# Decoder tail on one Trainium2 core: row lists of the last batch from one-hot products, kept experts' first weights loaded in the mixer, four gather buffers cleared before the block, rows weighted directly behind silu

## The reference

```python
logits = x @ gate_weight.T                      # 128 experts, 80 of them masked out
probs = softmax(where(old_to_new == -1, -inf, logits))
top_v, top_i = top_k(probs, 8); top_v = top_v / top_v.sum(-1)
flat_e = old_to_new[top_i]                      # kept expert of each (token, choice)
pos = running count of its expert, in token order
valid = pos < 192                               # capacity of an expert
gate_up = rows_of_expert @ gate_up_proj[e].T    # 512 -> 384
out = (silu(g) * u) @ down_proj[e].T            # 192 -> 512
final[token] += out * top_v   where valid
x = layernorm(x + final)
```

## Time and profile before

| | us |
|---|---|
| median of 3 timed runs | 2152.34 |
| lowest, highest | 2149.24, 2153.65 |
| the profiled execution's own time | 2148.72 |
| its span | 2147.0 |
| PE busy | 1748.3 (81%) |
| DVE busy | 1482.3 (69%) |
| POOL busy | 1083.6 (50%) |
| ACT busy | 957.9 (45%) |
| granted TensorE clock, mean | 0.887 |

### The profile page before, as it was taken

How to read it: one execution, slowest core, us unless ns; L and a number is a source line. 1 busy time by engine, 2 the same in 40 slices (tenths; PEclk the granted TensorE clock), 3 DMA queues, 4 the chain that set the end, 5 groups by cost and what they waited for, 6 DMA issues and landing times. The chain is left out here.

```text
span 2147.0 us, 34548 instructions
## 1 busy us (share of the span) xinstructions
PE 1748.3 (81%) x9164; PEld 1395.6 (65%) x9165; DVE 1482.3 (69%) x2836; ACT 957.9 (45%) x1867; POOL 1083.6 (50%) x816
## 2 busy tenths in 40 slices
PE   4898989347999999999998898697851179999990
PEld 3566665236889888888887556464531178888880
DVE  4466867764777888887886323857679557777774
ACT  4354452312444444444443323535333157777773
POOL 1000715464667667667676000036357757777763
PEclk9898989666999999999999899887865589999995
DMA  8011011034888888888986623131010469999967
GB/s 325 27 40 59 20 59 40 1 102 141 209 212 212 206 220 225 219 219 216 232 228 134 224 39 59 44 74 59 1 59 1 170 179 256 258 248 258 256 150 255
DMA packets 138551, 318.72 MB, mean 148 GB/s; under 512 B 30840, under 2 KB 31320, under 8 KB 136824
## 3 DMA queue, kind: packets, MB, share of 16 engines
q1 hardware_dynamic: 71448, 201.68, 27.1%
q0 software_dynamic: 64752, 112.04, 26.9%
q10 hardware_dynamic: 2288, 4.29, 0.5%
HBM read 238.61 MB, written 97.62 MB: 157 GB/s over the span
## 5 line engine op out<-in xcount | busy, mean ns | idle before, releaser
L98 POOL DMA_INDIRECT tab_rows<-pair,slot x256 | 313.9, 1226 | 450.7 <-DVEq L752 299.3
L90 PE MATMUL gu<-wgu_h,xgT_h 128*128 x648 | 233.5, 360 | 7.2 <-DVE xgT_l L1428 3.6
L1253 POOL DMA_INDIRECT xg<-x_rows,ids x167 | 191.6, 1148 | 62.3 <-issue 48.5
L90 PE MATMUL gu<-wgu_l,xgT_h 128*128 x648 | 219.4, 339 | 0.0
L90 PE MATMUL gu<-wgu_h,xgT_l 128*128 x648 | 218.3, 337 | 0.0
L1308 ACT ACTIVATE ysb<-yp,wts 128x512 f32<-128x512 f32 x160 | 110.3, 689 | 144.6 <-PE yp L1535 144.6
L90 PE MATMUL guk<-xgT_hk,wgu_hk 128*128 128x192 f32 x576 | 161.2, 280 | 0.0
L90 PE MATMUL guk<-xgT_lk,wgu_hk 128*128 128x192 f32 x576 | 158.4, 275 | 0.0
L1298 ACT ACTIVATE sg<-gu 128x192 f32<-128x192 f32 x162 | 53.7, 331 | 234.4 <-PE gu L90 234.4
L90 PE MATMUL guk<-xgT_hk,wgu_lk 128*128 128x192 f32 x576 | 158.2, 275 | 0.0
L1428 DVE TENSOR_TENSOR xgT_l<-tpx,xgT_h 128x512 fp32r<-128x512 f32 x163 | 112.2, 688 | 54.4 <-ACT xgT_h L1294 52.2
(11 more groups left out here) (500 smaller groups left out, 5108.1 us busy)
## 6 DMA issues: line engine op xcount, KB each, us to landing
wgu_sb<-in_wgu SPq DMA_DIRECT2D x64, 768.0 KB
wgu_sbk<-in_wgu SPq DMA_DIRECT2D x48, 768.0 KB, 4.4
wd_sb<-in_wd SPq DMA_DIRECT2D x64, 256.0 KB
wd_sbk<-in_wd SPq DMA_DIRECT2D x48, 256.0 KB, 5.2
ct<-in_ctxT SPq DMA_DIRECT2D x8, 1024.0 KB, 4.9
wd_sb<-in_wd SPq DMA_DIRECT2D x64, 128.0 KB
wd_sbk<-in_wd SPq DMA_DIRECT2D x48, 128.0 KB, 5.8
odd_rows<-zero SPq DMA_DIRECT2D x1, 4352.0 KB, 15.5
```

The source lines that it names most:

```text
L90: i = nc.tensor.matmul(out, left(k), right(k), start=(start and k == 0 and m == 0), stop=(k == ops - 1 and m == 2))
L98: nc.gpsimd.indirect_dma_start(out=tab, out_offset=bass.IndirectOffsetOnAxis(ap=s["slot"][:, n:n + 1].bitcast(U32), axis=0), in_=s["pair"] ...
L1253: nc.gpsimd.indirect_dma_start(out=xg[:, t % G, :], out_offset=None, in_=x, in_offset=bass.IndirectOffsetOnAxis(ap=ids[:, t:t + 1].bitcast ...
```

## The change

Four edits. (1) In the last batch no slot numbers and no scatter: all four tiles are routed at once; `own` is the one-hot of each of the 32 choices, and for each choice n two products, `spots[:, n, :]` (a one-hot of the position, 192 wide) transposed times `parts[:, n, :, :]` (the one-hot of the expert times five values: 1, token number, and the weight in three bf16 pieces), sum up on PE to the list entries of the last batch. The table holds the first three batches; it is loaded by SP, transposed as before, and both are added into `ids` and `wts` inside `mixer_two`. (2) SP loads experts 0 to 2 of `kept_experts` inside `mixer_two`, as soon as the last attention output is out; the buffers live over both blocks. (3) Gather buffers 0 to 3 are a tensor that lives over both blocks and is cleared behind the spots; 4 to 7 are cleared at the head of `kept_experts`, and only the gathers into them wait for it. (4) In ACT's loop both `weighted` stand directly behind silu, ahead of `h_upper` and `rest_upper`.

```diff
+def kept_weights(sp, d, s, e, gate_up, down):
+    loaded = s["kept_loaded"][e % 2]
+    if e >= 2:
+        sp.wait_ge(loaded, e // 2 * 48)
+    sp.dma_start(gate_up, d["wgu1"][e * P:(e + 1) * P, :, :]).then_inc(loaded, 16)
+    sp.dma_start(down[:, 0, :], d["wd1"][e * INTER:e * INTER + P, :]).then_inc(loaded, 16)
+    sp.dma_start(down[0:IR, 1, :], d["wd1"][e * INTER + P:(e + 1) * INTER, :]).then_inc(loaded, 16)
@@ kept_experts, SP
-            for e in range(E1):
+            for e in range(NR, E1):
...
@@ kept_experts, POOL
-            scatter(nc, tab, s, E1 * REG1 - 1, s_lot, BT - 1)
             def gather(t):
                 if t >= GK:
                     pool.wait_ge(s_xT, t - GK + 1)
+                elif t >= G and t % 2 == 0:
+                    pool.wait_ge(s_clear, (t - G) // 2 + 1)
...
-            pool.wait_ge(s_tab, 3)
@@ kept_experts, ACT, step
                         silu(g + (n + 1) // NF, (n + 1) % NF)
+                    weighted(g, 2 * n, not first or n >= G // 2)
+                    weighted(g, 2 * n + 1, not first or n >= G // 2)
+                    if not (last and n + 1 >= NF):
                         h_upper(g + (n + 1) // NF, (n + 1) % NF)
-                    weighted(g, 2 * n, not first or n >= G // 2)
-                    if not (last and n + 1 >= NF):
                         rest_upper(g + (n + 1) // NF, (n + 1) % NF)
-                    weighted(g, 2 * n + 1, not first or n >= G // 2)
...
-            act.wait_ge(s_lot, SCAT)
-            nc.scalar.dma_start(lot[:, :, :].rearrange("t n o -> t (n o)"),
-                                tab.rearrange("(r n) o -> r (n o)", n=P)[0:T1, :]).then_inc(s_rows, 16)
@@ kept_experts, DVE
-            nc.vector.memset(xg[:, :, :], 0.0).then_inc(s_tab, 1)
+            for n in range((GK - G) // 2):
+                nc.vector.memset(xg_late[:, 2 * n:2 * n + 2, :], 0.0).then_inc(s_clear, 1)
...
@@ mixer_two, SP, last step
+                        sp.wait_ge(s_op, 2 * B * BT)
+                        for e in range(NR):
+                            kept_weights(sp, d, s, e, s["wgu"][:, e * KC:(e + 1) * KC, :], s["wd"][:, e * 2:e * 2 + 2, :])
+                        sp.wait_ge(s_scat, (B - 1) * (16 * BT * TOPK))
+                        sp.wait_ge(s_rin, 2 * B * BT)
+                        sp.wait_ge(s_xT, B * KC)
+                        sp.dma_start(lot.rearrange("t n o -> t (n o)"),
+                                     d["tab1"].rearrange("(r n) o -> r (n o)", n=P)[0:T1, :]).then_inc(s_lot, 16)
                     sp.wait_ge(s_x5, b * BT + BT)
@@ mixer_two, POOL
-            for j in range(BT - 1):
-                pool.wait_ge(s_idx, B + j + 1)
-                scatter(nc, d["tab1"], drain, E1 * REG1 - 1, s["lot"][1], j, j + 1)
...
@@ mixer_two, DVE, last batch
+                def routed():
+                    dve.wait_ge(s_lg, (B - 1) + (ROUTED + BT))
+                    routing = route_rows(c, range(BT), mm[:, :, 0:E1])
+                    next(routing)
+                    next(routing)
+                    c.done(nc.vector.tensor_tensor(own, row[:, :].unsqueeze(1).to_broadcast([P, NP, E1]),
+                                                   en16[:, :].unsqueeze(2).to_broadcast([P, NP, E1]), ALU.is_equal))
...
+                        for src, n, out in ((ours, 4, fours), (fours, 2, pairs), (pairs, 1, mask[:, :, :].unsqueeze(2))):
+                            c.done(nc.vector.tensor_tensor(out, src[:, :, 0:n, :], src[:, :, n:2 * n, :], ALU.add))
...
+                def parts_made():
...
+                    c.done(nc.vector.tensor_tensor(parts[:, :, 1:NV, :], own.unsqueeze(2).to_broadcast([P, NP, NV - 1, E1]),
+                                                   values[:, :, :].unsqueeze(3).to_broadcast([P, NP, NV - 1, E1]), ALU.mult))
+                    dve.wait_ge(s_lot, 16)
+                    c.done(nc.vector.tensor_copy(lotf, lot[:, :, 0]))
+                def spots_made():
...
+                    for n in range(NP):
+                        nc.vector.tensor_scalar(spots[:, n, :], places[:, :], pos8[:, n:n + 1], None, ALU.is_equal).then_inc(s_spot, 1)
+                    c.done(nc.vector.memset(s["xg"][:, :, :], 0.0))
+                def lists_taken():
+                    dve.wait_ge(s_list, 1)
...
-                for j in range(BT):
-                    route_j(j)
-                    slots_j(j)
+                routed()
+                parts_made()
+                spots_made()
+                lists_taken()
@@ mixer_two, PE, last batch
+                for n in range(NP):
+                    pe.wait_ge(s_spot, n + 1)
+                    for m, (lo, w) in enumerate(((0, P), (P, IR))):
+                        nc.tensor.matmul(tb[0:w, m, 0:NV * E1].rearrange("p (v e) -> p v e", e=E1), spots[:, n, lo:lo + w],
+                                         parts[:, n, :, :], start=(n == 0), stop=(n == NP - 1))
+                nc.tensor.transpose(tp[:, 0, 0:T1], lotf, ident[0:T1, 0:T1])
+                nc.tensor.transpose(tp[:, 1, 0:T1], lot[:, :, 1].bitcast(F32), ident[0:T1, 0:T1]).then_inc(s_list, 1)
```

More of the change, by code:

```diff
@@ L2007, in _ @@
             load_ct(0)
-            sp.wait_ge(s_empty, 3)
+            sp.wait_ge(s_empty, 5)
             sp.wait_ge(s_set, 6)
@@ L2448, in drained @@
                 stat, mv, rstd, shift = stats[2]
+                own = parts[:, :, 0, :]
+                ours = own.rearrange("p (j k) e -> p j k e", k=TOPK)
                 c.done(nc.vector.tensor_scalar(tokf[:, :], tokf[:, :], float(S), None, ALU.add))
+                c.done(nc.vector.tensor_scalar(back[:, :], s["tcol"][:, 0:1], -1.0, -float(2 * P), ALU.mult, ALU.add))
                 dve.wait_ge(s_x4, B * BT)
@@ L2493, in drained @@
                 scaled(3)
-                for j in range(BT):
-                    route_j(j)
-                    slots_j(j)
-                with nc.allow_low_precision("small counts"):
-                    for j in range(BT):
-                        c.done(nc.vector.tensor_tensor(s["macc1"][:, :], s["macc1"][:, :], mask[:, j, :], ALU.add))
-                        c.wait()
+                routed()
+                parts_made()
+                spots_made()
+                lists_taken()
             norm1(0, True)
```

192 lines of the change are left out of this document (112 added, 80 removed).

## The result

The changed kernel takes 2159.01 us (median of 20 runs, 2134.60 to 2165.86), the kernel before 2151.28 (20 runs): ratio 1.0032, 95% interval 1.0019 to 1.0045. It is slower by 0.3%; the forecast was 2115. The profiled execution took 2165.7 us, span 2163.9.

A forecast was written before the change was run, and what follows sets the result against it. Two limits: PE's hole before the expert loop, waiting for routing and scatters, and an ACT-DVE ring in the loop. Gains 20.1 + 13.6 + 2 = 35.7 off 2148.72 gave 2113.0, plus 2 made 2115 us; range 2105 to 2131.

The forecast's parts named there:

- Part 5: Expert loop: weighted rows leave the ACT-DVE ring, 7.60 to 7.30 us per expert over 45 experts, gain 13.6 us.
- ACT-DVE ring: Expert loop: ACT and DVE wait for each other without slack, 7.68 us per expert, forecast to become 6.4.
- PE, or DMA: Expert loop: the next limit once the ring opens, PE at 7.20 us or DMA 98% busy; 7.30 taken.
- rival (c): Expert loop: add landings grow past the step and every expert waits; 2160 us at 8.3 per expert; chance 0.03.
- hole and head: PE's idle stretch before the expert block and that block's start: net gain 21.7 - 1.6 = 20.1 us.
- Part 3: List product in the hole: 64 products take 9.6 us, between 6.4 and 21, with weight loads hidden.
- Part 4: Head of the expert block: lists to first gate product takes 11.8 us against 10.2, a loss of 1.6.
- Part 6: Kernel end: last add about 2 us earlier against PE's end, gain 2 us.
- Routing: Last batch, all four tiles at once: mask ready 5.6 us after the logits, at 1676.5.
- The lists: In the hole: ready at 1701.4, 30.5 us after the last logits, 21.7 us earlier than before.

The follow-up runs named there:

- e16: Kernel before, with both adds of an expert going to one tensor and experts alternating between two tensors; ratio to before 0.9976.
- e17: Kernel before, with both weighted rows directly behind silu and both adds of an expert to one tensor, experts alternating between two; ratio to before 0.9886.
- e6: Changed kernel, with list products grouped by shape and only the even weighted row directly behind silu; ratio to before 0.9926.
- e8: e6 with the weights of experts 3 to 5 held until the first four gathered tiles landed; ratio to before 0.9929.
- e14: Changed kernel, with list products grouped by shape and both adds of an expert to one tensor, experts alternating between two; ratio to before 0.9810.
- e15: e14 with the weights of experts 3 to 5 held until four tiles are gathered; median 2105.77 us, ratio to before 0.9789.
- e10: Changed kernel, with list products grouped by shape and weights from expert 6 on held until h's lower part is made; ratio to before 0.9975.
- e12: Changed kernel: list products grouped by shape, adds before gathers, experts 3 to 5's weights held for four gathered tiles, later weights for h's lower part; ratio 0.9937.
- e5: Changed kernel, with both halves of the list product 128 columns wide, still alternating; one run, list product 8.60 us, loop 7.92 us per expert.
- e18: Changed kernel, with both adds of an expert to one tensor, experts alternating between two; ratio to before 0.9899.
- e3: Changed kernel, with adds going in turn to four tensors, half of the sum left out; ratio to before 0.9877.

## Why the prediction was wrong

**The step that failed is Part 5's gain**, "45 x (7.60 - 7.30) = 13.6; bounds 0 and 45 x 0.40 = 18", and with it the lower bound of 0 that the range rests on. The measured term is 45 x (7.60 - 7.99) = -17.6 us. Its first half was right: the ACT-DVE ring of 7.68 is what held the loop, and edit (4) opens it (e16 7.60, e17 7.22). What is late next was named wrongly as "PE, or DMA". It is rival (c), which the forecast described in place and mechanism ("L1650 waits for the add two before") and gave 0.03. It took the landing as fixed: "today a step of adds and landing is 5.53 us with an empty DMA and fits in 7.60 in the loop". In before's loop the same sum is 5.5 us for the odd add (4.7 and 0.8) and 6.3 for the even one (5.5 and 0.8), so the empty DMA was not the mistake for the odd add; the mistake was that this would hold once ACT's order sends both rows of an expert out early. Then it is 8.0. Part 5 itself ended on "adds and gathers do too" (come earlier) and drew nothing from it. The argument against (c), "the DMA work of an expert does not grow", looked at the share and not at the delay of one transfer: the share did not grow (0.92 against 0.93), the landing of the odd add went from 4.7 to 7.2 us. The price given there, 2160 at 8.3 us for an expert, was near for a wrong reason: 2159 at 7.99, because hole and head gave 4.4 us and not 20.1.

**Part 3, a mis-sized term**: 20.97 us for the list product instead of 9.6, 11.4 of the loss. "There the weight loads are hidden" came from position products, which all have 128 columns; the list products alternate between 128 and 64. The upper end of 21 was stated, and the middle was taken. With one shape at a time it is 9.24 to 9.8, with the clock rising inside, as forecast.

**Part 4, the head, a mis-sized term**: from the lists (1716.46) to the transposes of expert 2 (1737.99) are 21.5 us, against 15.3 before (1723.11 to 1738.38): 6.3 us dearer, where 1.6 were forecast. To the first gate product, as the forecast counted, it is 15.6 us (1716.46 to 1732.02) instead of 11.8. "The gather ... is hidden beside it unless expert 3's weights delay it by over 2 us": they did. The first gather landed 5.7 us after its issue (1717.79 to 1723.48), before 3.4 (1724.00 to 1727.44), and without the weights of experts 3 to 5 in the way the head is 4 to 5 us shorter (e6 to e8 4.9, e14 to e15 4.2).

**Part 6, the end, a mis-sized term**: 0.3 us (66.6 to 66.3) where 2 were forecast. The last add is issued 1.4 us earlier against PE's last transposes (the even one 19.8 us behind them in place of 21.3), and the adds of experts 45 and 46 wait for their weighted rows, not for a landing.

**What held.** Routing: mask ready at 1680.4, 5.6 us after the logits' end at 1674.8, as forecast; one-hot 1.76, adds 0.56, 0.36, 0.26 for 1.75, 0.55, 0.35, 0.25; `parts` 6.56 for 6.55; spots 5.83, within 3 to 6; the reduction 1.75, not the strided 2.7. Here the Trainium skill's rule on the doubled rate ("VectorE: DVE Perf Modes", section "What auto-detection actually checks") was weighed in the forecast, and the trace agrees with it: a still operand in 16 bits does not get it. The lists took 41.7 us from the logits' end to the last list row at 1716.46, where 30.5 were summed; the difference is the product's 11.4, less 0.2 elsewhere.

**The sum again, by e15**, which has the two repairs and the hold: hole and head 67.55 to 47.0, 20.5 us (forecast 20.1); loop 45 x 0.36 = 16 (forecast 13.6); end 2.0 (forecast 2). That the first and the last come so near the forecast is luck in part. 4.2 us of the 20.5 come from holding the weights, which the forecast did not have; without the hold it is 16.4 (e14). The 2.0 at the end come from the new wait rule: it alone gives 3.0 (e16). The gain of edit (4) in the loop was there and covered by a ring one step behind the one removed, and 11 us of the hole were covered by the shape of a product.

**What stays open.** What makes an add land after 5 us in one loop and after 7 in another was not found; in the changed loop gathers and weights land later too, and e10 to e12 only show that the wait moves. Of the first comparison's 7.7 us, the terms (hole and head -4.4, loop +17.6, end -0.3) give 12.9; with the 4.0 us ahead of the last logits that is the 16.9 between the two spans, and the profiled execution was 6.7 us above its kernel's median, where that of the kernel before was 2.6 below. So the terms belong to two single executions that lie further apart than the medians, and 7.99 may be on the high side for the changed kernel; e5, with the same order and the same wait, has 7.92.

## What to carry to other kernels

When a ring is opened, write down every ring next to it with its slack in the loop, and ask whether the new order leaves its length as it is: here the landing grew from 4.7 to 7.2 us with the same bytes per expert and the same DMA share. A rival that has place and mechanism deserves more than a few per cent when its length was taken as fixed. A wait for an accumulating DMA is worth a look at which rows must not meet: choosing the tensor by expert instead of by tile gave each landing twice the time. It took the changed kernel from 1.0032 to 0.9899 of before (e18), some 29 us, and it took the kernel before, whose loop does not wait there, only to 0.9976 (e16). And on PE, group small products by shape.

## What the runs showed of the hardware

- Products of 240 columns that alternate between 128 and 64 stationary columns: 0.31 and 0.34 us apart, clock 0.50 for all 21 us; in two groups, or all with 128: 8.6 to 9.8 us, clock 1.00 at their end.
- An indirect add of 64 rows landed in 4.7 us (median) or 7.2, in loops with the same bytes per expert and nearly the same DMA share (0.93, 0.92). In the changed kernel the next add that waited for it began 0.8 us after the landing.
- With 3.4 MB of weights held back until four tiles were gathered, PE's wait for the second pair of tiles went from 3.76 us (changed kernel) to 1.17 (e15).
- With the adds unchained the 16 DMA engines ran at 0.98 and 269 GB/s for 280 us (e3), and PE kept 7.28 us per expert.
